# Cross-attention and feed-forward layer on one core: queries projected ahead and kept in DRAM, keys by plain selections, constants laid out by the host, a new order of steps

## The reference

```python
def _L0_xattn_ref(x, y, mask, Wq, bq, Wk, bk, Wv, bv, Wo, bo, num_heads):
    q = (x @ Wq + bq).reshape(Bx, Tq, num_heads, d)
    k = (y @ Wk + bk).reshape(Bx, Tkv, num_heads, d)
    v = (y @ Wv + bv).reshape(Bx, Tkv, num_heads, d)
    att = scale * jnp.einsum('bthd,bThd->bhtT', q, k)
    att = att * mask - 10000000000.0 * (1.0 - mask)
    att = jax.nn.softmax(att, axis=-1)
    out = jnp.einsum('bhtT,bThd->bthd', att, v).reshape(Bx, Tq, Emb)
    return out @ Wo + bo
...
x = x + _L0_xattn_ref(_layernorm(x), ctx_1024, mask, ...)
# t = _layernorm(x); y = t + relu(t @ w1[0] + b1[0]) @ w2[0] + b2[0]
# x = x + (y - mean(y)) * rsqrt(var(y) + 1e-5) * gamma + beta
```

## Time and profile before

| | us |
|---|---|
| median of 3 runs | 248.0 (247.46 to 249.1) |
| the profiled execution | 246.66 |
| its span, first to last instruction | 244.9 |
| TensorE busy | 208.8 |
| VectorE busy | 149.8 |
| ScalarE busy | 120.9 |
| GpSimd busy | 80.2 |
| bytes moved by DMA | 26.09 MB |

### The profile page before, as it was taken

One profiled execution on the slowest core, in us unless ns is written; L12 is line 12 of the kernel. 1 busy time (PEld: TensorE's weight loads), 2 busy tenths in 40 slices (PEclk: granted clock), 3 DMA queues, 4 the chain that ended last, 5 costly groups with the idle time before them and its releaser, 6 DMA issues.

```text
span 244.9 us, 3545 instructions
## 1 busy us (share of the span) xinstructions
PE 208.8 (85%) x1273; PEld 159.0 (65%) x1273; DVE 149.8 (61%) x354; ACT 120.9 (49%) x210; POOL 80.2 (33%) x88
## 2 busy tenths in 40 slices
PE   0378779459968999996999999999999999889990
PEld 0273757145613775484779876898777899878890
DVE  1989478836651697442338865826858426885464
ACT  2442932326636447677632648744755850158200
POOL 5627617130410041824101732321541441460010
PEclk9999955959995799999999999999999999999998
DMA  6963679857767707593072434000410100011011
GB/s 180 364 212 77 182 175 244 223 173 190 174 152 215 167 19 130 139 197 118 5 160 78 111 66 107 3 3 26 106 45 4 43 0 3 0 43 43 3 43 43
DMA packets 18098, 26.09 MB, mean 107 GB/s; under 512 B 2441, under 2 KB 9393, under 8 KB 18081
## 3 DMA queue, kind: packets, MB, share of 16 engines
q1 hardware_dynamic: 15024, 20.85, 34.5%
...
## 4 chain that ended last, share of the span: by engine, by line
PE 61%; DMA 14%; DVE 12%; SPq 3%; issue 3%; ACT 2%; ACTq 2%; POOL 1%; POOLq 0%
PE T L674 7%; PE acc L686 6%; DMA Sq<-nmx 5%; PE W L736 5%; PE W L738 5%; PE M L654 5%; PE W L737 5%; PE W L753 4%; PE W L750 4%; PE W L751 4%; DMA Sq<-mD 3%; PE W L695 3%; SPq L520 2%; DMA xin<-in_x_dram 2%; DMA Mq<-qh 2%
## 5 line engine op out<-in xcount | busy, mean ns | idle before, releaser
L839 ACT ACTIVATE PT<-T 77x512 f32<-77x512 f32 x64 | 35.1, 592 | 35.8 <-PE T L674 28.3
L750 PE MATMUL W<-w2h,hh 128*128 128x256 f32 x128 | 36.5, 285 | 0.4 <-ACT hh L883 0.4
L994 DVE TENSOR_REDUCE mx<-M 128x6 f32<-128x462 f32 (+1 forms) x48 | 26.1, 580 | 17.4 <-PE M L654 17.1
L753 PE MATMUL W<-w2h,hl 128*128 128x256 f32 x128 | 36.2, 283 | 0.2 <-DVE hl L1057 0.2
L751 PE MATMUL W<-w2l,hh 128*128 128x256 f32 x128 | 36.0, 281 | 0.0
L674 PE MATMUL T<-Sq,KS 128*77 128x512 f32 x64 | 26.2, 470 | 6.3 <-ACT PT L839 3.7
L879 ACT ACTIVATE hr<-W,cols 128x512 f32<-128x512 f32 x32 | 22.1, 689 | 12.3 <-PE W L738 11.1
L654 PE MATMUL M<-KM,Mq 128*128 128x234 f32 (+1 forms) x96 | 21.3, 346 | 7.6 <-DMA Mq<-qh 6.5
L736 PE MATMUL W<-x2h,w1h 128*128 128x512 f32 x64 | 26.3, 410 | 1.5 <-DVE x2l L1051 1.5
L654 PEld LDWEIGHTS M<-KM,Mq 128*128 128x128 f32 (+1 forms) x96 | 17.9, 240 | 13.7 <-DMA Mq<-qh 7.9
L1176 POOL TENSOR_TENSOR hl<-hr,hh 128x512 fp32r<-128x512 f32 x12 | 15.5, 1288 | 33.0 <-ACT hh L883 33.0
...
## 6 DMA issues: line engine op xcount, KB each, us to landing
...
```

The source lines that it names most:

```text
L750: e.matmul(y, hh[:, f, q:q + 128], w2h[:, f * E:(f + 1) * E], start=(f == 0), stop=False)
L753: i = e.matmul(y, hl[:, f, q:q + 128], w2h[:, f * E:(f + 1) * E], start=False, stop=(f == 7))
L839: e.activation(PT[:, m % 6, :], T[m % 2][0:TK, :], ACT.Exp).then_inc(exped, 1)
L994: e.tensor_reduce(heads, M[(nth[step] - 1) % 2][:, 0:w * KP].rearrange("p (g h t) -> p g h t", g=1 if s < 2 else 2, t=KP)[:, :, :, 0:TK], ...
```

## The change

**Queries.** `xn`, `xnT` are double, `qh` has four parts, so the queries of a chunk can be made while the chunk before is still at its maxima; the order makes all of them in the first third (`qproj` due 13.7 to 51.1). Each high part is stored to qD once, and each low part once, in steps `qproj` and `qlow` of SP; ScalarE issues no DMA after the start. qD has the shape (heads, 16, 2, 512). Sq's query rows are loaded in two DMAs per quad (high and low interleaved, high again). Mq is loaded from qh for chunk 0 and from qD for the others. bq comes in by a third product with the mask's flag rows (bqr and mT).

**Keys.** The products of bq with the keys and the rows for them are gone. KM takes one product a head, KS two, with selections sel_m, sel_h, sel_l made by ScalarE; identity rows come from a constant `eye`, as the rows of Mq, Sq, KM and KS are laid out anew (64 of mask, 48 of queries, 13 of mask, maxima, flags).

**Constants.** The host lays out the biases bq, bk, bv, b1 in the constant (128 x 476) and passes the context turned (ctx_t). Both, with wk and wv, are loaded on ScalarE's queue. Rows of x go to partitions in fours (4 KB in one piece); all four chunks of x are loaded at the start.

**Mask of the second half.** `maskm` and `masks` are two steps each, for the slots that are free first.

**Maxima.** `mx` is double. The number of turns of the maxima of a chunk is a function, `turns(c)`, which gives 2 for each chunk: halves, as before.

**End.** `finish` is split: `centre` no longer waits for the root. The order is new for all engines.

```diff
 D = 16
 TK = 77
 KP = 78
-FR = 77
-MR = 79
-QR = 80
+Q0 = 64
+Q1 = 112
+MR = 125
+FR = 126
 F = 1024
 EPS = 1e-5
...
-        "turn": "11.3 / 31.9 / 53.7 / 81.6",
-        "qproj": "14.2 16.0 / 34.3 36.5 / 56.5 58.8 / 88.6 107.1",
...
-        "mxt": "30.5 36.1 / 50.5 56.1 / 75.6 86.8 / 146.0 148.6",
...
+        "turn": "11.5 / 19.6 / 27.5 / 43.1",
+        "qproj": "13.7 16.7 / 21.5 24.4 / 31.4 34.5 / 45.0 51.1",
...
+        "mxt": "30.8 37.2 / 47.9 56.0 / 71.6 79.5 / 96.9 121.8",
...
+        "norm": "4.6 / 10.7 / 19.3 / 36.3",
+        "scale": "9.1 / 16.9 / 24.3 / 41.2",
...
+        "qproj": "18.6 23.6 / 27.2 33.7 / 35.6 45.7 / 50.2 53.9",
...
+        "keys": "21.8 27.9 29.4 30.7 31.4 33.2",
...
+        "split": "48.9 50.9 52.3 53.1",
+        "smax": ("22.4 23.0 26.0 26.6 28.5 29.0 29.9 30.3 32.0 32.6 34.4 35.0 / 38.8 39.4 40.0 40.6 43.6 44.1 44.5 45.2 "
+            "47.7 48.3 49.6 54.6 / 57.5 58.8 59.9 62.1 66.7 67.1 70.0 70.4 71.6 72.2 74.2 74.8 / 77.4 81.2 81.8 83.7 "
+            "86.2 89.9 90.4 92.0 99.1 102.6 107.3 119.9"),
...
-        "qproj": "18.2 20.8 / 41.6 42.9 / 61.1 63.7 / 92.6 111.1",
-        "qload": "16.8 19.5 / 38.1 40.3 / 59.8 62.4 / 91.3 109.8",
-        "quadq": "22.8 23.2 46.3 49.1 / 59.0 65.0 67.7 77.9 / 80.9 86.3 107.3 121.4 / 126.8 132.9 157.1 162.0",
-        "quadm": "39.4 39.9 46.8 49.5 / 59.4 65.4 68.1 77.4 / 93.9 94.3 106.8 121.0 / 148.7 149.1 156.6 161.5",
...
+        "statics": "40.5",
+        "maskm": "49.7 56.0",
+        "masks": "66.6 78.7",
+        "qproj": "19.3 24.4 / 25.5 35.2 / 39.9 53.2 / 55.4 63.7",
+        "qlow": "19.9 24.9 / 32.6 41.8 / 42.3 48.5 / 54.9 61.5",
+        "qload": "17.7 22.7 / 34.1 38.3 / 51.6 57.1 / 74.3 76.5",
+        "quadq": "26.0 28.7 37.2 42.9 / 47.4 53.8 58.2 62.0 / 75.4 77.6 83.4 87.8 / 102.6 109.1 113.4 123.9",
+        "quadm": "32.1 33.2 39.4 41.2 / 51.0 52.7 60.9 63.1 / 73.7 79.8 84.5 88.9 / 103.7 110.2 123.3 125.0",
...
+            for c in (2, 3):
+                e.dma_start(xin[:, 4 * c:4 * c + 4, :], x_v[:, row0(c)]).then_inc(ld_x[c], 16)
...
+                    fresh.wait_ge(mT_made, 2)
...
                 elif kind == "maskm":
+                    i, = a
+                    n, first = ((4, 0), (2, 4))[i]
                     fresh.wait_ge(m_out, 16)
-                    fresh.wait_ge(scored, 24)
-                    e.dma_start(Mqf[0:QR, :, :], mD[:, 512:1024].unsqueeze(1).to_broadcast([QR, 6, 512])
-                                ).then_inc(ms_static, 16)
+                    fresh.wait_ge(scored, nth["smax", 1, 3, 1 + i])
+                    for p, q in ((0, Q0), (Q1, MR)):
+                        e.dma_start(Mqf[p:q, first:first + n, :], mD[p:q, :].unsqueeze(1).to_broadcast([q - p, n, 512])
+                                    ).then_inc(ms_new[i], 16)
                 elif kind == "masks":
+                    i, = a
                     fresh.wait_ge(m_out, 16)
-                    fresh.wait_ge(st_made, 32)
-                    e.dma_start(Sqf[0:QR, :, :], mD[:, 512:1024].unsqueeze(1).to_broadcast([QR, 8, 512])
-                                ).then_inc(sq_static, 16)
+                    fresh.wait_ge(st_made, nth["st", 1, 11 + 4 * i])
+                    for p, q in ((0, Q0), (Q1, MR)):
+                        e.dma_start(Sqf[p:q, 4 * i:4 * i + 4, :], mD[p:q, :].unsqueeze(1).to_broadcast([q - p, 4, 512])
+                                    ).then_inc(sq_new[i], 16)
                 elif kind == "qproj":
                     c, g = a
-                    qd = qD[c][8 * g:8 * g + 8]
+                    fresh.wait_ge(q_high, nth[step])
+                    e.dma_start(qD[c][8 * g:8 * g + 8, :, 0, :].rearrange("h d n -> (h d) n"),
+                                qh[:, 2 * (c % 2) + g, :].bitcast(F32)).then_inc(qh_out[2 * (c % 2) + g], 16)
+                elif kind == "qlow":
+                    c, g = a
                     fresh.wait_ge(q_split, nth[step])
-                    e.dma_start(qd[:, 1, :, :], ql[:, g, :].bitcast(F32)).then_inc(q_out[g], 16)
...
                 elif kind == "qload":
                     c, g = a
-                    fresh.wait_ge(q_high, nth[step])
-                    if c:
-
-                        fresh.wait_ge(scored, 12 * (c - 1) + (12 if g else 8))
-                    for j in range(2):
-                        e.dma_start(Mqf[QR:P, 2 * g + j, :],
-                                    qh[48 * j:48 * j + 48, g, :].bitcast(F32)).then_inc(ms_ld[g], 16)
-                    e.dma_start(Mqf[QR:QR + 32, 4 + g, :], qh[96:P, g, :].bitcast(F32)).then_inc(ms_ld[g], 16)
+                    if c == 0:
+                        fresh.wait_ge(q_high, nth["qproj", c, g])
+                        fresh.wait_ge(ms_static[g], 3)
+                        for j in range(2):
+                            e.dma_start(Mqf[Q0:Q1, 2 * g + j, :],
+                                        qh[48 * j:48 * j + 48, g, :].bitcast(F32)).then_inc(ms_ld[g], 16)
+                        e.dma_start(Mqf[Q0:Q0 + 32, 4 + g, :], qh[96:P, g, :].bitcast(F32)).then_inc(ms_ld[g], 16)
+                    else:
+                        fresh.wait_ge(qh_out[2 * (c % 2) + g], 16 * (c // 2 + 1))
+                        fresh.wait_ge(scored, nth["smax", c - 1, 3, 1])
+                        e.dma_start(Mqf[Q0:Q1, 2 * g:2 * g + 2, :],
+                                    qD[c][8 * g:8 * g + 6, :, 0, :].rearrange("(j h) d n -> (h d) j n", j=2)
+                                    ).then_inc(ms_ld[g], 16)
+                        e.dma_start(Mqf[Q0:Q0 + 32, 4 + g, :],
+                                    qD[c][8 * g + 6:8 * g + 8, :, 0, :].rearrange("h d n -> (h d) n")).then_inc(ms_ld[g], 16)
...
                     u, s = quad(c, k), 4 * (k % 2)
-                    fresh.wait_ge(q_out[k // 2], 48 * (c + 1))
-                    if u > 1:
+                    fresh.wait_ge(qh_out[2 * (c % 2) + k // 2], 16 * (c // 2 + 1))
+                    fresh.wait_ge(ql_out[k // 2], 16 * (c + 1))
+                    if u < 2:
+                        fresh.wait_ge(sq_static, 4 * u + 4)
+                    else:
                         fresh.wait_ge(st_made, 4 * (u - 1))
-                    e.dma_start(Sqf[QR:P, s:s + 4, :],
-                                qD[c][4 * k:4 * k + 4].rearrange("h r d n -> (r d) h n")).then_inc(sq_ld[u % 2], 16)
+                    heads = qD[c][4 * k:4 * k + 4]
+                    e.dma_start(Sqf[Q0:Q0 + 32, s:s + 4, :], heads.rearrange("h d r n -> (d r) h n")).then_inc(sq_ld[u % 2], 16)
+                    e.dma_start(Sqf[Q0 + 32:Q1, s:s + 4, :],
+                                heads[:, :, 0, :].rearrange("h d n -> d h n")).then_inc(sq_ld[u % 2], 16)
...
                     u, s = quad(c, k), 4 * (k % 2)
-                    fresh.wait_ge(nmx_made, nth["mxt", c, k // 2])
-                    if u > 1:
+                    fresh.wait_ge(nmx_made, turned_by(c, k))
+                    if u < 2:
+                        fresh.wait_ge(sq_static, 4 * u + 4)
+                    else:
                         fresh.wait_ge(st_made, 4 * (u - 1))
-                    fresh.wait_ge(sq_static, 8 + 16 * (c // 2))
-                    e.dma_start(Sqf[MR:QR, s:s + 4, :], nmx[s:s + 4, k // 2, :].bitcast(F32)).then_inc(sq_ld[u % 2], 16)
+                    source = nmx[s:s + 4, k // 2, :] if turns(c) == 2 else nmx[4 * k:4 * k + 4, c % 2, :]
+                    e.dma_start(Sqf[MR:MR + 1, s:s + 4, :], source.bitcast(F32)).then_inc(sq_ld[u % 2], 16)
...
                     fresh.wait_ge(ld_wq, 16)
                     t = take(step)
-                    e.matmul(t[:, :], wq[:, 0, g * 128:(g + 1) * 128], xnT[:, 0, :], start=True, stop=False)
-                    e.matmul(t[:, :], wq[:, 1, g * 128:(g + 1) * 128], xnT[:, 1, :],
+                    e.matmul(t[:, :], wq[:, 0, g * 128:(g + 1) * 128], xnT[:, c % 2, 0, :], start=True, stop=False)
+                    e.matmul(t[:, :], wq[:, 1, g * 128:(g + 1) * 128], xnT[:, c % 2, 1, :], start=False, stop=False)
+                    fresh.wait_ge(bqr_made, 1)
+                    fresh.wait_ge(mT_made, half(c) + 1)
+                    e.matmul(t[:, :], bqr[:, g, :], mT[:, 512 * half(c):512 * half(c) + 512],
                              start=False, stop=True).then_inc(q_made, 1)
...
-                        o = t[0:64, 2 * TK * j:2 * TK * (j + 1)]
...
+                    for i, h in enumerate(range(3 * j, min(3 * j + 3, 8))):
+                        o = t[0:48, 2 * TK * i:2 * TK * (i + 1)]
                         high = kh[:, g, :, :].rearrange("p b t -> p (b t)")
-                        e.matmul(o, single[0:TK, 8 * g + h, :], low[0:TK, :, :].rearrange("p b t -> p (b t)"),
-                                 start=True, stop=False)
                         if to == "KM":
-                            i = e.matmul(o, once[:, h, :], high, start=False, stop=True)
+                            made = e.matmul(o, sel_m[:, h, :], high, start=True, stop=True)
```

(42 more changed lines are left out.)

488 lines of the change are left out of this document (224 added, 264 removed), and 160 rows, old and new, of the table TIMES.

## The result

The changed kernel takes **226.6 us** (median of 4 runs, 223.5 to 228.1) beside 248.3 for the kernel before, measured with it (247.5 to 249.1): ratio 0.9085, 95% interval 0.8987 to 0.9183. It is faster, and 2.2 us above the forecast of 224.4. The profiled execution took 226.6 with a span of 224.8.

A forecast was written before the change was run, and what follows sets the result against it. TensorE was taken as the bound after 120 us, with 47 us lost, mostly earlier. First transposed score 39.5 + work left 162.6 + loss 15 + tail 5.5 + 1.8 gave 224.4 us; likely 218 to 231, bounds 214 to 238.

The forecast's parts named there:

- TensorE's work: Whole kernel: instruction counts times pace at 2.4 GHz give 186 us, unchanged, with 162.6 left at the first transposed score.
- First score at 23.5: Head: constants laid out by the host bring chunk 0's first score of the maxima to 23.5 us from 30.5, bounds 22 to 27.
- First transposed score at 39.5: After chunk 0's first maxima: their row, issued ahead of chunk 1's query loads, allows it at 39.5 us against 52.7, bounds 36 to 46.
- 15 us lost after it: TensorE's loss from the first transposed score to its end: 15 us against 22.5 before, bounds 8 to 22.5.
- the lead that was to hide the way through DRAM: Queries of chunks 1 to 3: made a chunk ahead, hiding the store; without that lead, 2 to 4.5 us once per chunk.
- only the head is won: Rival: first score at 23.5, but later stretches lose as before because the DMA queue is as full; 238 us, chance 0.10.
- the long wait was one of order on SP: Before the first transposed score: maxima ready at 38.6 were issued at 46.7 because SP stood in chunk 1's query loads.
- The ScalarE issues: After the first transposed score: removing 16 DMA issues from ScalarE takes about 4 us off the path.
- VectorE (233): Rival: VectorE bounds the first 80 us, its 66 us of steps ending at 89; 233 us, chance 0.15.
- SP's queue (279): Rival: SP issues nearly all DMAs and becomes the bound, at 1.85 us per issue 279 us; chance 0.05.
- Packed at once: Rival: less idle time up front keeps TensorE's clock high from 40 us, loss 8 instead of 15; 217 us, chance 0.12.
- Port: About 10 to 30 us: VectorE and GpSimd share a port, making 3 or 4 VectorE operations 1 us longer, the sum some 3 higher.

The follow-up runs named there:

- run 2: The changed kernel without reloading the mask rows of the second half (chunks 2 and 3 use the first half's mask): 217.75 us, ratio 0.8705.
- run 7: The changed kernel with the 8 stores of the queries' high parts issued by ScalarE again instead of SP: 224.4 us, ratio 0.9098.
- runs 5 and 6: The kernel before, chunk 0's negated maxima issued ahead of chunk 1's query loads; the second also moves four transposed scores up: 254.1 and 255.3 us.
- run 4: The changed kernel's instructions, stores and layouts with chunk steps in the kernel before's order, put together and untuned: 253.0 us, ratio 1.0111.
- run 3: The changed kernel with each maximum taken over 39 of the 77 keys only: 226.2 us, ratio 0.9054.
- c_qload: The changed kernel with SP storing and loading chunk 1's second half of queries earlier, next to the first half: 221.7 us, ratio 0.8874.
- c_q_no_reload: The changed kernel with chunk 1's queries stored and loaded earlier on SP and no mask-row reload for the second half: 215.7 us, ratio 0.8687.

## Why the prediction was right

**TensorE's work** (186 us, 162.6 left at the first transposed score) is a count at the upper clock, and nothing contradicts it: with it 219.8 - 36.7 - 162.6 gives the loss behind that point, 20.5 us.

**First score at 23.5** was 22.7, inside 22 to 27, by errors that cancel: the first queries were cast at 19.2, not 17.5 (TensorE starts at 9.0, not 5.9, as its first product waits for wk on ScalarE's queue), but their three loads took 1.9 us to issue, not 2.5, and had landed at most 1.5 us after the last of them, not 4.5. That it came out within 1 us is luck.

**First transposed score at 39.5** was 36.7. The maxima were negated by 34.5 (I had 34.2) and SP issued at once, but the row was in Sq 2.2 us after the start of its issue, where I had 0.6 for the issue and 4.5 for a landing taken from another load.

**15 us lost after it was 20.5: the mis-sized term.** I had 5.3 steady, at most 5 for the lower clock, some 4 for DMA waits at the chunk changes. The lower clock cost about 3.5 (0.86 over 25 us), and the DMA waits were 10.6: 5.5 for rows of maxima, 5.1 for queries. The 6.4 that are left stand against the 5.3; they were not taken apart. In the 5.1 is one that the prediction had named: the lead that was to hide the way through DRAM is gone for the second half of chunk 1's queries, cast by 32.2, stored from 37.41 and loaded from 41.20. Under "only the head is won" I had written that landings of 4.5 to 6 us come from traffic, which falls only a little, and then put it aside because "the long wait was one of order on SP". It was both. In the new order the transfers are bunched, behind SP's stand of 9.1 us as well as by the denser work: the DMA share is 0.94 in 62 to 85 (0.74 before in the same window) but only 0.65 in 37 to 62 (0.81 before), and the reload that the forecast counted as hidden "earlier, under chunk 1's products" costs 226.6 - 217.8 = 9 us by run 2. The ScalarE issues, counted as 4 us won, show no gain: with eight of them back the time is the same (run 7). The terms of the sum that were wrong in the other direction, 2.8 us at the first transposed score and 0.5 at the tail (5.0 for 5.5), brought the total back to within 2.2 us of the forecast, which is luck too; the range of 214 to 238 held without it.

**The step on order** failed as worded. The row's wait from 38.6 to 46.7 was put down to SP's loads of the next queries alone; GpSimd's copy into the last slot of Sq held it to 43.8 as well, and moving SP's issues in the kernel before made it no faster (runs 5 and 6). That the gain needs the new order as a whole fits run 4; it isn't isolated, since that run's order has a fault of its own.

**Rivals.** VectorE (233): refuted by run 3, in which 9.9 us less of maxima change nothing. Only the head (238): refuted by the first transposed score at 36.7. SP's queue (279): an issue takes 0.3 to 0.65 us also at a DMA share of 0.94, against the 1.3 at which it would have decided; the 1.85 of the earlier trace rows stood beside ScalarE's own issues. "Packed at once" (217): a_no_reload (217.8) comes near to it and c_qload (221.7) half way, each by taking away one of the two causes; c_q_no_reload, with both away, is at 215.7 with the full clock nearly throughout (mean 0.995).

**Port.** The scaling of chunk 2 took 3.69 us, with GpSimd busy all along beside it (23.4 to 28.4):

```profile
9.53 1.72 DVE L949 TENSOR_SCALAR xn<-xin,x_mv,x_rs 128x256 f32<-128x256 f32 x4 [0.27 <-POOL x_rs L1145]
...
24.87 3.69 DVE L949 TENSOR_SCALAR xn<-xin,x_mv,x_rs 128x256 f32<-128x256 f32 x4
```

The same four instructions took 1.72 at 9.5. That is what the prediction weighed, 2 us of it in one place. It did reach TensorE: two maxima stand behind this scaling in VectorE's order, and TensorE waits 1.08 us for them at 29.3. It didn't reach the first transposed score: with the shorter maxima of run 3 the row was issued 1.35 us earlier (33.17) and landed only 0.3 earlier (36.45), since it lands with what was issued before it.
